# Softmax division moved behind PV in the last attention, and smaller pieces of vector work in the first

## What is computed

```python
x = L0(x, mask, ctx, mask)      # attention along channels; mean and deviation of v; (xn * std + mean) * mask
x = L1(ctx, x, mask2)           # latents attend to ctx and themselves; MLP
x = L2(x, ctx, ctx)             # two cross attentions of width 16 x 128; MLP
x = L3(x, ctx, mask3)           # below

# L3
x = layer_norm(hidden_states, ln1_w, ln1_b)
q, k, v = heads(x @ q_w + q_b), heads(ctx @ k_w + k_b), heads(ctx @ v_w + v_b)
attn = softmax(where(mask, einsum('bhqd,bhkd->bhqk', q, k) / sqrt(16), min), axis=-1)
out = einsum('bhqk,bhkd->bhqd', attn, v).reshape(B, LQ, D) @ cproj_w + cproj_b
hidden = out + hidden_states
return hidden + gelu(layer_norm(hidden, ln2_w, ln2_b) @ fc_w + fc_b) @ proj_w + proj_b

# L0, the norm of x with its mask (n_valid of each row)
mean = sum(x * m) / n_valid;  var = sum((x * m)**2) / n_valid - mean * mean
xn = (x - mean) / sqrt(relu(var) + EPS) * m
```

## Time and profile before

| | us |
|---|---|
| median of 3 runs | 1174.37 |
| lowest, highest | 1172.15, 1174.82 |
| the profiled execution, its own time | 1175.04 |
| its span in the trace | 1173.2 |
| granted TensorE clock, mean of the span | 0.978 |

### The profile page before, as it was taken

The page is one execution under the profiler, slowest core; times in us unless marked ns, Lnnn a source line. Parts: engine busy times, 40 slices in busy tenths (PEclk is TensorE's granted clock), DMA queues, the critical chain, the costliest instruction groups (busy, mean ns, idle before and its releaser), DMA issues.

```text
span 1173.2 us, 24063 instructions
## 1 busy us (share of the span) xinstructions
PE 1062.5 (91%) x8248; PEld 936.7 (80%) x8248; DVE 727.7 (62%) x1747; ACT 715.2 (61%) x2080; POOL 317.5 (27%) x440
## 2 busy tenths in 40 slices
PE   7998897789978999999998989999999989778788
PEld 5776675677758979999998868999998979667588
DVE  7777574667886645555555645555555585667773
ACT  2776765677884456666655546666665452689852
POOL 5232543756540012211111103111112112143311
PEclk9999899899999999999999999999999999899899
DMA  5211011011101021111001101011111110100100
GB/s 171 66 46 41 22 43 33 15 23 27 45 20 53 19 90 46 46 46 46 19 29 68 46 1 57 35 46 46 46 46 37 37 54 1 48 18 19 48 10 28
DMA packets 29853, 48.09 MB, mean 41 GB/s; under 512 B 6627, under 2 KB 20389, under 8 KB 29734
## 3 DMA queue, kind: packets, MB, share of 16 engines
q1 hardware_dynamic: 29638, 46.49, 12.7%
q10 hardware_dynamic: 96, 0.07, 0.0%
HBM read 36.54 MB, written 1.05 MB: 32 GB/s over the span
## 4 chain that ended last, share of the span: by engine, by line
PE 66%; DVE 12%; ACT 10%; issue 7%; POOL 2%; SPq 1%; DMA 1%; ACTq 0%; DVEq 0%; POOLq 0%
PE ps L764 14%; PE ps L765 14%; PE ps L766 14%; PE ps L1008 4%; PE ps L984 4%; PE ps L1146 3%; ACT pt L1270 2%; PE ps L993 2%; PE ps L909 2%; DVE nm L1806 2%; PE ps L1133 1%; PE ps L1124 1%; PE ps L932 1%; DVE nmax L1609 1%; POOL pt L1857 1%
## 5 line engine op out<-in xcount | busy, mean ns | idle before, releaser
L1857 POOL TENSOR_TENSOR pt<-pt,prec 128x256 f32<-128x256 f32 (+1 forms) x224 | 180.8, 808 | 628.2 <-DVE prec L1678 500.4
L1325 ACT ACTIVATE pt<-ps,nmax 128x129 f32<-128x129 f32 x256 | 92.1, 366 | 101.0 <-DVE nmax L1670 100.2
L764 PE MATMUL ps<-rs 128*128 128x256 f32 x480 | 142.8, 298 | 4.1 <-DVE rs L1692 2.8
L1471 DVE TENSOR_TENSOR rs<-wraw,rs 128x256 fp32r<-128x256 f32 (+2 forms) x116 | 68.8, 595 | 124.5 <-ACT rs L1201 124.1
L765 PE MATMUL ps<-rs 128*128 128x256 f32 x480 | 135.9, 283 | 0.0
L766 PE MATMUL ps<-rs 128*128 128x256 f32 x480 | 135.8, 283 | 0.0
L1270 ACT ACTIVATE pt<-ps,nmax 128x256 f32<-128x256 f32 (+1 forms) x256 | 105.1, 423 | 42.6 <-DVE nmax L1609 42.3
L764 PE MATMUL ps<-ht,rs 128*128 128x256 f32 (+1 forms) x304 | 107.6, 354 | 9.0 <-DVE ht L1521 3.0
L766 PE MATMUL ps<-ht,rs 128*128 128x256 f32 (+1 forms) x304 | 101.4, 333 | 0.0
L765 PE MATMUL ps<-ht,rs 128*128 128x256 f32 (+1 forms) x304 | 101.3, 333 | 0.0
L764 PEld LDWEIGHTS ps<-rs 128*128 128x128 f32 x480 | 91.8, 191 | 7.9 <-DVE rs L1692 4.8
(11 more groups left out here) (206 smaller groups left out, 2998.8 us busy)
## 6 DMA issues: line engine op xcount, KB each, us to landing
wraw<-in_packs SPq DMA_DIRECT2D x52, 512.0 KB, 3.8
rs<-rs SPq DMA_DIRECT2D x222, 32.0 KB, 1.9
bvr<-in_l2rows SPq DMA_DIRECT2D x16, 256.0 KB, 4.6
rs<-rs SPq DMA_DIRECT2D x96, 16.0 KB
row<-in_rows SPq DMA_DIRECT2D x2, 640.0 KB, 4.9
XH<-in_packs SPq DMA_DIRECT2D x2, 512.0 KB, 4.0
out<-X SPq DMA_DIRECT2D x4, 256.0 KB, 2.1
X<-in_x SPq DMA_DIRECT2D x3, 256.0 KB, 3.3
```

What stands on the lines that cost most here:

```text
L764: nc.tensor.matmul(dst, w[0], m[1], start=start, stop=False)
L1325: last = nc.scalar.activation(prob[:, g % PROBS, k * D:k * D + P + 1], ps[:, S_BANK + g % 2, k * D:k * D + P + 1], ACT.Exp, bias=nmax[:, g ...
L1471: last = nc.vector.tensor_tensor(dst[1], src, f32(dst[0]), ALU.subtract)
L1857: nc.gpsimd.tensor_tensor(pr, pr, prec[:, u % 4, 0:nh].unsqueeze(2).broadcast_to([P, nh, keys]), ALU.mult)\
```

## The change

It has three parts, and all of them are changes of order or form; what is computed stays the same.

**Division behind PV (last attention only).** The exponentials write no sums. `PV` has the transposed probabilities as weights (128 columns) and moves the values, 16 channels and a column of ones, so that the 17th column of its result is the row sum. A new DVE step `NO`, once for each two units, takes the reciprocal of eight sums and multiplies the eight heads into a new tile `attn`. `OUT` is now a PE step too: four transposes of `attn` into bank 6 or 7, from which ACT and DVE split as before. POOL's 32 products, DVE's 32 reciprocals of 128x4, and the wait of `T` for them go; `T` waits for the exponential. `OUT` and `WO` come later in the list. The values need two additions of 128x256 in place of four of 128x128, and POOL writes two columns of ones in place of the zeroed tile.

**First attention in pieces.** The `xs` steps of sequences 1 to 7 go from ticks 10, 20, ... 70 to 10, 26, 30, 42, 46, 58, 62; the six factors become steps of their own at ticks 74 to 79; each `res` becomes two steps of one sequence, two ticks apart.

**Second norm group behind unit two.** `nT L3n1 1` moves from ahead of the first unit to behind the second, and `pk` goes ahead of `pq` in the first step.

```diff
@@ first_order
         if b:
-            put(10 * b, "xs", b)
+            put((10, 26, 30, 42, 46, 58, 62)[b - 1], "xs", b)
+    for k in range(6):
+        put(74 + k, "xf", k)
-    for k, (dev, mul, res, lat) in enumerate([(84, 91, 95, 119), (None, 93, 99, 123), (150, 152, 155, 160), (None, 154, 158, 164)]):
+    for k, (dev, mul, res, lat) in enumerate([(84, 91, 95, 119), (None, 93, 99, 123), (150, 152, 155, 160), (None, 154, 159, 164)]):
...
-        put(res, "res", k)
+        for half in range(2):
+            put(res + 2 * half, "res", k, half)
@@ att_order
     if ph == "L3":
+        put(1, "nT", "L3n1", 1)
...
-    for _, e, k in prep:
+    for _, e, k in prep if ph == "L1" else prep[::-1]:
         yield (e, 0, k)
-    if ph == "L3":
-        yield ("nT", "L3n1", 1)
...
-            if w % per_it == per_it - 1:
+            if ph == "L1" and w % per_it == per_it - 1:
                 yield ("OUT", w // per_it)
+        if ph == "L3" and 2 <= w <= total and w % 2 == 0:
+            yield ("NO", w // 2 - 1)
+        for it in range(c["iters"] if ph == "L3" else 0):
+            if w == (it + 1) * per_it + (2 if it + 1 < c["iters"] else 0):
+                yield ("OUT", it)
@@ PE
                 elif e == "T":
-                    pe.wait_ge(a["nm"], i + 1)
+                    pe.wait_ge(a["nm" if ph == "L1" else "ex"], i + 1)
...
+                elif e == "PV" and ph == "L3":
...
+                    if i >= 4 and im == 0:
+                        pe.wait_ge(a["nm"], i // 2 - 1)
+                    for q in range(4):
+                        last = nc.tensor.matmul(sums(i // 2)[:, im, q, 0:HD + 1], probT[:, i % 3, q * P:(q + 1) * P],
+                                                vt[:, it % 2, im, 0, 4 * m + q, 0:HD + 1], start=True, stop=True)
+                    last.then_inc(a["pm"], 1)
+                elif e == "OUT" and ph == "L3":
+                    pe.wait_ge(a["nm"], STEPS * (i + 1))
+                    bank = j_bank()
...
@@ ACT
+                        if ph == "L1":
+                            last = nc.scalar.activation(p_h, s_h, ACT.Exp, bias=nmax[:, i % 4, h:h + 1], accum_out=psums[:, i % 4, h:h + 1])
+                        else:
+                            last = nc.scalar.activation(p_h, s_h, ACT.Exp, bias=nmax[:, i % 4, h:h + 1])
@@ DVE
+                elif e == "NO":
+                    it, m = divmod(i, STEPS)
+                    dve.wait_ge(a["pm"], 2 * i + 2)
...
+                    link(nc.vector.reciprocal(rc, sums(i)[:, :, :, HD]))
...
+                    nc.vector.tensor_tensor(dst, sums(i)[:, :, :, 0:HD], rc.unsqueeze(3).broadcast_to([P, 2, 4, HD]),
+                                            ALU.mult).then_inc(a["nm"], 1)
...
                 elif e == "res":
-                    two = slice(2 * i, 2 * i + 2)
+                    b = 2 * i + k[0]
@@ POOL
                 if e == "S":
-                    normalise(a, i, 4 // U, keys, keys)
+                    if ph == "L1":
+                        normalise(a, i, 4 // U, keys, keys)
```

More of the change, by code:

```diff
@@ L33 @@
 H = 16
+HD = D // H
 DK2 = 128
@@ L593, in copied, with sums @@
                 eng.wait_ge(A[ph]["teD"], i - i // n)
+        def sums(s):
+            return ps[:, O_BANK + s % 2, 0:2 * P].rearrange("p (m q c) -> p m q c", m=2, q=4)
         def dense_keys(ph, part, it, m):
@@ L835, in prep @@
                 it, m = divmod(s, STEPS)
-                if s == 0 and e == "pq":
+                if s == 0 and e == ("pq" if ph == "L1" else "pk"):
                     pe.wait_ge(a["mask"], 1)
@@ L911, in att @@
                     last.then_inc(a["tm"], 1)
+                elif e == "PV" and ph == "L3":
+                    it, r = divmod(i, 2 * STEPS)
+                    m, im = divmod(r, 2)
+                    copied(pe, ph, i)
+                    if r == 0:
+                        pe.wait_ge(a["vals"], it + 1)
+                    if i >= 4 and im == 0:
[7 more added lines that the diff above has]
+                    bank = j_bank()
+                    for im in range(2):
+                        for t in range(2):
+                            last = nc.tensor.transpose(bank[:, (2 * im + t) * P:(2 * im + t + 1) * P], attn[:, i % 2, im, t * P:(t + 1) * P],
+                                                       ident[:, :])
+                    j_full(last, (a["oeA"], i + 1), (a["oeD"], i + 1))
                 elif e == "PV":
@@ new lines, in x_stats @@
+                link(nc.vector.tensor_tensor_reduce(ms[:, 0, b, :], X[:, b, :], mt8[:, b, :], 1.0, 0.0, ALU.mult, ALU.add,
+                                                    sd[:, 3, b:b + 1]))
+                last = nc.vector.tensor_tensor_reduce(ms[:, 1, b, :], ms[:, 0, b, :], ms[:, 0, b, :], 1.0, 0.0, ALU.mult, ALU.add,
+                                                      sd[:, 4, b:b + 1])
+                if b == B - 1:
+                    link(last)
+                else:
+                    last.then_inc(l0stat, 1)
@@ new lines, in x_factors @@
+            def x_factors(k):
+                if k == 0:
+                    link(nc.vector.reciprocal(sd[:, 2, :], sd[:, 2, :]))
+                elif k == 1:
+                    link(nc.vector.tensor_tensor(mv[:, :, 0], sd[:, 3, :], sd[:, 2, :], ALU.mult))
+                elif k == 2:
+                    link(nc.vector.tensor_tensor(sd[:, 4, :], sd[:, 4, :], sd[:, 2, :], ALU.mult))
+                elif k == 3:
+                    link(nc.vector.tensor_tensor(sd[:, 5, :], mv[:, :, 0], mv[:, :, 0], ALU.mult))
+                elif k == 4:
+                    link(nc.vector.tensor_tensor(sd[:, 4, :], sd[:, 4, :], sd[:, 5, :], ALU.subtract))
+                else:
+                    nc.vector.tensor_scalar(sd[:, 0, :], sd[:, 4, :], 0.0, None, ALU.max).then_inc(l0stat, 2)
@@ L1973, in _ @@
                 add_row(X, "L2b2", b)
[L1974 to L1975 removed]
+                if b < 2:
+                    ones = nc.gpsimd.memset(vt[:, b, :, 0, :, HD], 1.0)
+                if b == 1:
+                    ones.then_inc(vzero, 1)
             pool.wait_ge(M["L2m"]["out"], B // 2)
```

78 lines of the change are left out of this document (36 added, 42 removed).

## The result

The changed kernel takes 1190.01 us (median of four, 1188.05 to 1192.67) where the kernel before took 1173.26 in the same comparison: a ratio of 1.0147, 95% interval 1.0118 to 1.0176. The forecast was 1168. The page of its profiled execution (1188.05 us) begins as follows; PEclk is the granted clock of TensorE in 40 slices.

What follows compares the result with a forecast made beforehand. No engine bounds all of the last attention: ACT leads the first and last eight units, PE comes nearest between. -3.4 - 1.5 - 2.9 = -7.8, one given back: 1175.0 - 6.8 = 1168.2, less 0.7; named 1168, range 1160 to 1178.

Steps and rivals of the forecast that it cites:

- rival D: Last attention from unit 8 on: few moved columns let the granted clock fall; +6, 1181 us, chance 0.12.
- The end: Behind the last PV: division (0.5) and four transposes (0.5) come ahead of the network's matmuls; about +1.3 us.
- PV: Last attention: eight pieces with 128-column loads take 0.88 us a unit, idle pieces go; +0.36 us of PE's time.
- The stages: Last attention: units 0 to 7 -2.0, 8 to 15 -0.7, 16 to 23 +1.3, 24 to 31 -1.0, rest +1.0.
- the middle units take 24 us or more: Last attention, sign of a wrong forecast: PE's waits don't shrink when PE is later; only the first layer's gain stays.
- The exponentials do start 0.25 to 0.26 apart: Last attention, ACT: without reads of sums exponentials start 0.25 us apart, saving 0.36 a unit, 11.5 over 32 units.
- The sum: All terms: -3.4 - 1.5 - 2.9 = -7.8 us, one microsecond given back for banks, leaving -6.8.
- First layer, statistics: First attention: factors one at a time between maxima remove PE's 2.38 us wait and the slow PV group; -3.4 us.
- First layer, result rows: First attention: result rows in halves shorten PE's 2.40 us wait; -1.5 us, between -2.6 and +1.6.
- Start: Start of the last attention: the norm's second group behind unit two falls into PE's waits; -1.5 us, between 0 and -2.1.
- DVE: Last attention: 32 reciprocals (5.4 us) go, 16 divisions of some 0.5 (8 us) come; hidden while PE or ACT is late.

## Why the prediction was wrong

**The clock (rival D).** This is the step that failed. The prediction named the mechanism and gave it 0.12, against it "the middle stages have 1.00 and PE will have fewer waits". Fewer waits were taken as protection. They didn't protect: PE was busy 8.55 of 10.30 us ahead of the fall, no smaller a share than the 20.15 of 24.93 at 1.00 before, and behind it 10.14 of 10.14 us at 0.50. The same waits with 119 columns bring no fall, and 12.3 us come back. D's size was near: it put 27 us of the way from unit 8 on at the lower level, and the granted clocks of the rows give, as an estimate, 27 of 91.7. That way takes 83.2 us with 119 columns, 8.5 less, where D had 13; the first units and the end give back 2.8 more. The Trainium skill (TensorE: Matmul & The Clock Gate, What's actually happening) has the clock follow how busy PE has been. By the busy time of a profile the trace disagrees: 10.14 of 10.14 us busy at 0.50. Whether the chip counts something else as busy, no run here shows.

**The end.** +1.3 forecast, +7.0 measured. The working counted division and transposes behind PV as if nothing stood between. It did not read where the last division stands on DVE: behind the network's conversion, which waits for a GELU. Moved, the end costs +4.1 at the lower clock, and +2.4 at the upper one.

**PV.** 0.88 us a unit forecast, and right at the upper level: from the end of the transposes' loads (1023.88 + 0.46) to the next step's load (1025.20) it is 0.86 us, and no idle piece stands around it. At the lower level eight pieces take 1.71 (1032.14 to 1033.85), which the sum did not hold. By the Trainium skill (TensorE: Matmul & The Clock Gate, Back-to-back issue gap) eight pieces would take 0.65; no run shows that.

**The stages.** Units 16 to 23, at 1.00 before and after, were to take 22.9 and take 24.41 us. PE's own time was right: 22.4 forecast, 22.33 of loads measured. The term that failed is the waits. They were to shrink from 2.5 us to 0.5, "since ACT returns 0.36 and PE comes 0.36 later", and they are 2.1 (below: total, times, longest). The prediction's own sign for this, "the middle units take 24 us or more", came true. Half the loads takes 3.6 us off PE's loads there and only 1.3 to 1.7 off the stage.

```profile
PEld ps L869 <- issue: 1.1, 2, 0.9
PEld ps L862 <- DVE rs L1621: 0.5, 1, 0.5
PEld ps L862 <- issue: 0.3, 1, 0.3
```

With wide columns, units 8 to 15 take 23.2 to 23.7 (24.2 forecast), and units 24 to 31 take 20.8 (19.4 forecast). Units 0 to 7 were to take 20.6 and take 23.44, or 22.05 with wide columns. The exponentials do start 0.25 to 0.26 apart, as forecast: four of 0.37 us (in the groups further below) take 1.14 on ACT's timeline.

```profile
1057.73 1.14 ACT L1306 ACTIVATE pt<-ps,nmax 128x128 f32<-128x128 f32 x4
```

But the time that ACT gets back reaches next to nobody. With the sums put back units 0 to 7 take 22.54, 0.5 more than the 22.05 without them, with wide columns and the same clock, and units 8 to 15 take 23.51, no more than the 23.2 to 23.7 without.

**The sum.** The prediction's parts of the attention, with the start, are +1.3 - 0.7 - 2.0 - 1.0 + 1.0 + 1.3 - 1.5 = -1.6, and not the -2.9 that it wrote: one +1.3 was left out. With it the forecast would have been 1169. The miss of 22 us doesn't hang on it.

**First layer, statistics.** -3.4 forecast, and alone -3.4 measured by the medians, -2.2 by the ratio, whose interval takes in the forecast. The mechanism was right: the wait of 2.38 us is gone, the PV group takes 1.86, as in the chain that ended last and in the ten microseconds of the earlier trace rows:

```profile
105.97 1.86 PE ps L1177 x32
```
```profile
100.00:110.00 10.00, 9.93 (x89) 7.99 (x88) 7.26 (x19) 7.68 (x16) 3.37 (x8) 1.00 0.13 32
```

**First layer, result rows.** -1.5 forecast, and alone +2.7 by the medians, +2.2 by the ratio. Half a pair was sized at 1.3 us; the first half takes 1.25 + 0.83, and two halves 3.48 where the pair took 2.54. With it comes a stretch of lower clock 130 us later, 1.5 us, which no term held. Why the clock falls there in these kernels and not in the others stays open.

**Start.** -1.5 forecast, -0.8 measured.

**DVE.** Reciprocal and product take 0.205 and 0.291 us, 0.5 as forecast, and hide except at the end. The groups of 1005 to 1140 (busy us, mean ns, idle before):

```profile
L1306 ACT ACTIVATE pt<-ps,nmax 128x128 f32<-128x128 f32 x128 | 36.5, 370 | 18.4 <-DVE nmax L1656 17.3
L1656 DVE TENSOR_REDUCE nmax<-ps 128x4 f32<-128x512 f32 x32 | 22.1, 690 | 37.2 <-PE ps L910 37.1
...
L1670 DVE TENSOR_TENSOR fs<-ps,prec 128x128 f32<-128x128 f32 x16 | 4.7, 291 | 0.6
...
L1668 DVE RECIPROCAL prec<-ps 128x8 f32<-128x8 f32 x16 | 3.3, 205 | 0.3
```

The maxima wait 37.1 us for PE's scores and the exponentials 17.3 for the maxima: PE stands at the head of the chain.

## What to carry to other kernels

Ask of a matmul that is turned round not only what its loads cost but how many columns it moves per load; where the bank has room, repeat the moving columns, which was free under the load here, and look at the granted clock. When a step moves to another engine, read what stands ahead of it in that engine's order at the last turn, where nothing else covers it. Before a gain in the first 100 us is believed, run it alone: positions in the traces of two executions differ by as much as the gain. And a wait is taken off the sum only when the step that ends it is known to come earlier.

## What the runs showed of the hardware

PE at 100% busy ran at 1.2 GHz for ten microseconds and more (10.14 of 10.14 us, 10.22 of 10.22) when a good part of its work was f32 pieces with 128-column loads and 17 moved columns. Ahead of the first of these stretches it had been busy 8.55 of 10.30 us at 2.4. With 119 moved columns and the same 8.51 of 10.20 us the level stayed at 2.4, and with 51 columns units 8 to 15 ran at 2.4 too. With 17 columns, 32-column loads and idle time between (18.78 of 24.75 us busy) it stayed at 2.4 as well. f32 pieces with 128-column loads follow each other every 0.11 us at 2.4 GHz and every 0.21 us at 1.2, and eight of them last 0.97 us whether each moves 17, 51 or 119 columns. The first eight units took no less time with the clock held at 2.4 (22.08 us against 22.05 with the lower level in it, 22.97 against 22.62): there other engines set the pace.
